# A graph-attention and mixture-of-experts layer: the last stage's three-way sum moved from ScalarE, GpSimd and VectorE to TensorE

## The reference

```
x = x + gnn(layernorm(x))                       # 4 heads of 64, 206,250 edges
x = x + ffn(layernorm(x))
# ffn: n = layernorm(x)
#   two experts of 16 per row, shares = softmax of the two gate values
#   moe = share0 * expert0(n) + share1 * expert1(n)
#   y   = n + moe
#   out = (y - mean(y)) / sqrt(var(y) + 1e-5) * gamma + beta
```

## Time and profile before

| | |
|---|---|
| runs | 2946.33, 2944.32, 2936.62 us; median 2944.32 us |
| profiled execution | 2945.44 us, its span 2943.7 us (first to last instruction) |
| mean granted TensorE clock | 0.796 of full speed |
| busy over the whole span | PE 76%, DVE 62%, POOL 64%, ACT 22% |
| expert stage ends (last matmul) | 2814.7 us from the span's start |
| last stage: first DMA issue to end of span | 2828.0 to 2943.7 us |

### The profile page before, as it was taken

How to read it: one execution, slowest core, us unless ns; L and a number is a source line. 1 busy time by engine, 2 the same in 40 slices (tenths; PEclk the granted TensorE clock), 3 DMA queues, 4 the chain that set the end, 5 groups by cost and what they waited for, 6 DMA issues and landing times. The chain is left out here.

```text
span 2943.7 us, 63652 instructions
## 1 busy us (share of the span) xinstructions
PE 2235.2 (76%) x10751; PEld 1884.9 (64%) x10752; DVE 1831.0 (62%) x4851; ACT 649.5 (22%) x2612; POOL 1887.7 (64%) x1912
## 2 busy tenths in 40 slices
PE   3588887888788888788787888887847368999920
PEld 2476776667666666666666766676637157999920
DVE  6666666666666666666666666666678851222258
ACT  1211111111111111111111111111112134555532
POOL 2277777777777777777777777777751344555533
PEclk9777778787778877887888788878875579999965
DMA  5355555555555555555555555555532056333356
GB/s 150 89 139 136 135 134 136 135 135 137 132 136 136 136 135 135 137 135 134 135 136 135 136 135 136 135 136 134 136 114 84 4 169 199 107 99 105 106 163 207
DMA packets 298512, 386.43 MB, mean 131 GB/s; under 512 B 104450, under 2 KB 235882, under 8 KB 298474
## 3 DMA queue, kind: packets, MB, share of 16 engines
q0 software_dynamic: 87744, 243.02, 31.9%
q10 hardware_dynamic: 84912, 75.49, 10.3%
q1 hardware_dynamic: 125818, 67.52, 8.3%
HBM read 351.08 MB, written 33.93 MB: 131 GB/s over the span
## 5 line engine op out<-in xcount | busy, mean ns | idle before, releaser
L552 POOL DMA_INDIRECT ring<-z_table,idx_ring x1612 | 1550.6, 962 | 495.6 <-issue 449.4
L738 PE MATMUL psMb<-msg,xs 128*128 128x260 f32 x3608 | 1208.2, 493 | 263.2 <-DVE msg L649 261.7
L738 PEld LDWEIGHTS psMb<-msg,xs 128*128 128x128 f32 x3608 | 829.1, 241 | 437.5 <-issue 271.3
L727 PEld LDWEIGHTS psEb<-nodes,xs 128*128 128x128 f32 x3608 | 566.4, 229 | 249.1 <-issue 214.8
L727 PE MATMUL psEb<-nodes,xs 128*128 x3608 | 532.8, 275 | 141.5 <-DVE xs L607 140.5
L649 DVE TENSOR_TENSOR msg<-ring,psPb 128x1024 f32<-128x1024 f32 x451 | 545.7, 1210 | 0.0
L621 DVE TENSOR_TENSOR earg<-es_edge,psEb 128x16 f32<-128x16 f32 x451 | 76.6, 170 | 604.2 <-ACT es_edge L699 599.2
L699 ACT COPY es_edge<-ring 128x16 f32 x451 | 91.9, 204 | 1493.4 <-SPq L523 1317.7
L613 DVE TENSOR_TENSOR xs<-iota_f,psPb 128x512 f32<-128x512 f32 x451 | 306.1, 679 | 1.4 <-ACT psPb L708 0.4
L607 DVE TENSOR_SCALAR xs<-dst_bc,iota_p 128x512 f32<-128x512 bf16 x451 | 231.7, 514 | 40.4 <-issue 20.4
L1224 DVE COPY xT<-psXd 128x256 f32<-128x256 f32 x108 | 45.8, 424 | 318.8 <-PE psXd L1158 318.8
(11 more groups left out here) (201 smaller groups left out, 1488.1 us busy)
## 6 DMA issues: line engine op xcount, KB each, us to landing
dst_bc<-dst_rows ACTq DMA_DIRECT2D x451, 128.0 KB
ring<-z_table,idx_ring POOLq DMA_INDIRECT x1612
w_all<-in_L_ffn_w_dram SPq DMA_DIRECT2D x32, 512.0 KB
b_sb<-in_L_ffn_b_dram ACTq DMA_DIRECT2D x108, 128.0 KB, 3.0
got<-pair_rows SPq DMA_DIRECT2D x48, 256.0 KB, 2.8
xs<-in_x_dram SPq DMA_DIRECT2D x6, 1536.0 KB, 13.8
idx_ring<-src_idx SPq DMA_DIRECT2D x403, 2.0 KB
z_table<-z_out SPq DMA_DIRECT2D x49, 130.0 KB, 1.9
```

The costliest lines, as they stand in the source:

```text
L552: nc.gpsimd.indirect_dma_start(ring[:, s, c, :], None, z_table, bass.IndirectOffsetOnAxis(ap=idx_ring[:, s, c:c + 1], axis=0)).then_inc(b_ ...
L727: last = nc.tensor.matmul(dest_of(s)[:, c * SH:(c + 1) * SH], ST[:, s, c * P:(c + 1) * P], nodes[:, bass.ds(tile, 1), :].rearrange("p o c ...
L738: last = nc.tensor.matmul(psM[s % 2][:, 0:ROW], S[:, s, c, :], msg[:, s, c, :], start=c == 0, stop=c == G - 1)
```

## The change

ACT no longer scales the rows. For each tile it makes two 128x128 matrices that hold the shares on their diagonals (`ident` times the share of each row, two activations at L1263 of the changed file). PE then makes the sum in PSUM with three float32 matmuls of 256 columns: diagonal 0 by the first expert's rows, diagonal 1 by the second's, and `ident` by the normed rows. There are two pairs of diagonals and four PSUM banks. DVE drops its addition and takes statistics and scale from PSUM; its statistics of tile t stand first in a turn, and `finish` follows `scale` directly. GpSimd has nothing left in the stage. SP's load waits for PE's sum in place of DVE's.

```
         with ExitStack() as ctx:
             got = sb(ctx, "got", [P, ER, TOP + 1, D])
             y = sb(ctx, "y", [P, ER, D])
+            diag = sb(ctx, "diag", [P, 2, TOP, P])
+            psS = [ps(ctx, f"psSe{i}") for i in range(4)]
...
-                def scale_first(t, s, r):
-
-                    act.wait_ge(e_got[s], 16 * 2 * (r + 1))
-                    nc.scalar.activation(got[:, s, 0, :], got[:, s, 0, :], ACT.Copy, scale=share[:, 0, bass.ds(t, 1)]).then_inc(e_first, 1)
-                pipeline(act, NT, ER, ER, [(scale_first, 0), (root, 3)])
-
-            @block.gpsimd
-            def _(pool):
-                def base(t, s, r):
-
-                    pool.wait_ge(e_first, t + 1)
-                    nc.gpsimd.tensor_tensor(got[:, s, 0, :], got[:, s, 0, :], got[:, s, TOP, :], ALU.add).then_inc(e_base, 1)
-                pipeline(pool, NT, ER, 0, [(base, 0)])
+                def spread_shares(t, s, r):
+
+                    if not early(t, 2):
+                        act.wait_ge(e_ps, t - 1)
+                    for k in range(TOP):
+                        last = nc.scalar.activation(diag[:, s % 2, k, :], ident[:, :], ACT.Copy, scale=share[:, k, bass.ds(t, 1)])
+                    last.then_inc(e_diag, 1)
+                pipeline(act, NT, ER, ER, [(spread_shares, 0), (root, 3)])
+
+            @block.tensor
+            def _(pe):
+                def combine(t, s, r):
+                    pe.wait_ge(e_diag, t + 1)
+                    pe.wait_ge(e_got[s], 16 * 2 * (r + 1))
+                    if not early(t, 4):
+                        pe.wait_ge(e_fin, 2 * (t - 4) + 2)
+                    for k in range(TOP):
+                        nc.tensor.matmul(psS[s % 4][:, 0:D], diag[:, s % 2, k, :], got[:, s, k, :], start=k == 0, stop=False)
+                    nc.tensor.matmul(psS[s % 4][:, 0:D], ident[:, :], got[:, s, TOP, :], start=False, stop=True).then_inc(e_ps, 1)
+                pipeline(pe, NT, ER, ER, [(combine, 0)])
...
-                def add_second(t, s, r):
-                    dve.wait_ge(e_base, t + 1)
-                    if not early(t, ER):
-                        dve.wait_ge(e_out[s], 16 * r)
-                    nc.vector.scalar_tensor_tensor(out=y[:, s, :], in0=got[:, s, 1, :], scalar=share[:, 1, bass.ds(t, 1)],
-                                                   in1=got[:, s, 0, :], op0=ALU.mult, op1=ALU.add).then_inc(e_sum, 1)
-
                 def tile_stats(t, s, r):
-                    dve.wait_ge(e_sum, 2 * t + 1)
-                    nc.vector.bn_stats(mv[:, s, 0:6], y[:, s, :]).then_inc(e_sum, 1)
+                    dve.wait_ge(e_ps, t + 1)
+                    nc.vector.bn_stats(mv[:, s, 0:6], psS[s % 4][:, 0:D]).then_inc(e_sum, 1)
...
-                pipeline(dve, NT, ER, ER, [(add_second, 0), (variance, 1), (invert, 2), (scale, 2), (tile_stats, 0), (finish, 2)])
+                pipeline(dve, NT, ER, ER, [(tile_stats, 0), (variance, 1), (invert, 2), (scale, 2), (finish, 2)])
...
                 def load(t, s, r):
                     if not early(t, ER):
-                        sp.wait_ge(e_sum, 2 * (t - ER) + 1)
+                        sp.wait_ge(e_ps, t - ER + 1)
```

More of the change, by code:

```diff
@@ L1241, in gnn_moe_kernel @@
         e_got = [sem(f"e_got{i}") for i in range(ER)]
-        e_sum = sem("e_sum"); e_fin = sem("e_fin"); e_var = sem("e_var"); e_root = sem("e_root")
-        e_first = sem("e_first"); e_base = sem("e_base"); e_y = sem("e_y"); e_out = [sem(f"e_out{i}") for i in range(ER)]
+        e_diag = sem("e_diag"); e_ps = sem("e_ps"); e_sum = sem("e_sum"); e_fin = sem("e_fin"); e_var = sem("e_var"); e_root = sem("e_root")
+        e_y = sem("e_y"); e_out = [sem(f"e_out{i}") for i in range(ER)]
         with ExitStack() as ctx:
@@ L1283, in variance @@
+                    nc.vector.bn_stats(mv[:, s, 0:6], psS[s % 4][:, 0:D]).then_inc(e_sum, 1)
                 def variance(t, s, r):
-                    dve.wait_ge(e_sum, 2 * t + 2)
+                    dve.wait_ge(e_sum, t + 1)
                     dve.sem_inc(apart, 1)
@@ L1292, in scale @@
                 def scale(t, s, r):
-                    nc.vector.scalar_tensor_tensor(out=y[:, s, :], in0=y[:, s, :], scalar=mv[:, s, 6:7], in1=affine[:, 0:D],
+                    if not early(t, ER):
+                        dve.wait_ge(e_out[s], 16 * r)
+                    nc.vector.scalar_tensor_tensor(out=y[:, s, :], in0=psS[s % 4][:, 0:D], scalar=mv[:, s, 6:7], in1=affine[:, 0:D],
                                                    op0=ALU.subtract, op1=ALU.mult).then_inc(e_fin, 1)
```

## The result

| | before | changed |
|---|---|---|
| median of 9 runs | 2944.32 us (2936.28 to 2949.18) | 2932.79 us (2927.24 to 2936.97) |
| ratio, 95% interval | | 0.9966 (0.9953 to 0.9979) |
| profiled execution, its span | 2945.44, 2943.7 us | 2927.24, 2925.5 us |

The change takes 11.5 us off the median. By the ratio it is 0.34%, 10.0 us, with an interval from 6 to 14 us. The forecast was 8.2 us, to 2937; that number starts from the profiled execution of 2945.44 us, and from the median the same 8.2 us give 2936.1. The same two kernels, compared once more (10 and 15 runs), gave 0.9960 (0.9948 to 0.9972).

The account below looks back on a forecast made before the run. VectorE was taken to bound the last stage at 2.084 us a tile, with SyncE's issues next. Start +0.5, steady part -9.0 and end +0.3 gave -8.2 us from 2945.44, so 2937 us, range 2929 to 2951.

Parts of the forecast that it names:

- forecast case: Last stage: turn of 1.80 to 1.92 us a tile, own range 2933 to 2941 us, chance 0.55.
- the rival in which DMA is the limit: Last stage: DMA engines, not SyncE's issues, set the pace at 1.72 us a tile, giving 2932 us; chance 0.15.
- the steady part: Last stage, 40 tiles going from 2.084 to 1.86 us each: 9.0 us less.
- VectorE bound, slowed by GpSimd: Last stage before: VectorE sets the pace, 1.64 us a turn with GpSimd idle, 0.44 more from overlap with GpSimd.
- SyncE is late next, at 1.84 us: Last stage after: SyncE's three DMA issues a tile set the turn, 1.84 us, bounds 1.75 to 1.95.
- DMA near its limit, so 0.02 more, 1.86: Last stage: DMA share would be 0.96 at 1.84 us, so 0.02 was added, making 1.86 us a tile.
- SyncE no limit: Last stage: SyncE's 0.71 us step contains a wait, DMA sets the pace at 1.72 us a tile, 2932 us; chance 0.15.
- VectorE's turn 1.34: Last stage: VectorE's turn without its addition, 1.24 us, plus 0.10 for finish waiting on scale; covered by SyncE.
- PSUM operands: VectorE's statistics and scale reading PSUM instead of SBUF: priced at 0, bounds -0.1 to +0.2 us a turn.
- TensorE's clock: Last stage: starts at 0.50, full some 5 us later and holds; at 0.50 again for the last tile.
- half-clock rival: Last stage: TensorE at half clock takes 2.67 us a tile, 2972 us; most or much of the stage, 2950 to 2972: 0.10.
- Start and end: Last stage: start priced +0.5 us (0 to +2), end +0.3 us (-1.1 if TensorE is at full clock).

Follow-up runs that it names:

- E3: Kernel before with GpSimd's addition of the normed rows left out, VectorE's addition kept, TensorE idle: 1.897 us a tile, stage 108.05 us.
- E5: Kernel before with GpSimd's addition of the normed rows done by VectorE, TensorE and GpSimd idle: 1.970 us a tile.
- E1: Changed kernel with the last stage's 49 stores issued by GpSimd instead of SyncE: 1.452 us a tile, stage 89.38 us, one run of 2920.96 us.
- E2: Changed kernel loading the normed rows of only 64 of 128 partitions, same count of DMA issues: 1.918 us a tile.
- E10: Changed kernel with GpSimd issuing stores, last tile split 96 and 10, VectorE's statistics between scale and finish: 1.360 us a tile, 0.9888 of the kernel before.
- E7: Changed kernel with only the first of TensorE's three matmuls a tile, all loads kept: 1.820 us a tile.
- E9: Changed kernel with only the first two of TensorE's three matmuls a tile, all loads kept: 1.835 us a tile.
- E4: Changed kernel with the last tile's loads and store split into 96 and 10 rows: load 48 to end 11.89 us against 20.91, 1.823 a tile.

## Why the prediction was right, and where its numbers were off

The median alone would not say so. At 2932.8 us it lies inside the whole range of 2929 to 2951, but just below the forecast case's own range of 2933 to 2941, and nearest to the 2932 of the rival in which DMA is the limit. The rows of the stage decide: SyncE's issues are the chain, and the stage is 9.3 us shorter where 8.2 were forecast. That 9.3 is so near to 8.2 is in part luck: the end, 0.6 us worse than forecast, hides part of the 1.6 us by which the steady part did better.

- **VectorE bound, slowed by GpSimd.** Right. E3 takes away only GpSimd's addition and gets 7.5 of 10.6 us; E5 shows the overlap as dearer than doing both additions in a row. Why the two engines slow each other, no run shows.
- **SyncE is late next, at 1.84 us.** Right in kind, shown by E1 (one issue less, pace 1.45) and supported by E2 (fewer bytes, no gain). The `ISA` row was priced at 0.06 us and was worth 0.10: 1.818 instead of 1.84. The turn without a jump, 1.76 us, is below the 1.80 to 1.90 that the prediction named as its sign and just above the 1.75 that it named as a sign of being wrong.
- **DMA near its limit, so 0.02 more, 1.86.** This step failed: no run shows the added term of 0.02 us a tile. The share of 0.85 at 2.084 us was scaled up as if 1.00 were a ceiling. E1 ran at share 1.06 and E10 at 1.08 and 373 GB/s, a pace of 1.36 us where the sum allowed 1.77, or 1.56 by the rate of loads alone. SyncE's turn, 0.02 us too long, and this 0.02 are the 0.04 us a tile by which 1.86 missed 1.818, and so the -9.0 that measured -10.6.
- **The rival "SyncE no limit".** Refuted in the direction of the forecast. The Trainium skill, "DMA: Bandwidth & Descriptors", section "Issuing engines are not separate DMA queues", has issue time as usually small beside the transfer. That did not hold in this stage: SyncE's turn of issues took 1.82 us, and the transfers of a tile can be done in 1.36 (E10).
- **VectorE's turn 1.34.** Too low. Finish right behind scale costs 0.61 us from start to start in the loop, not 0.50, and the turn is 1.48 (E1). It was covered by SyncE here; as soon as SyncE is relieved it is not, and the order of before gives 1.24 (E10). PSUM operands cost next to nothing: scale took 466 ns in the mean (494 before, some of them beside GpSimd) and the statistics 430 (414 before).
- **TensorE's clock.** As forecast: 0.50 at first, 1.00 four to five us later and through the steady part, 0.50 again for the last tile. The half-clock rival fell, and E7 says more: with SyncE at 1.82 us one matmul a tile at a level of 0.50 costs nothing, since it fits in. The Trainium skill, "TensorE: Matmul & The Clock Gate", section "A second HAM failure mode: psum-queue depth-cycling", has the clock swing in a kernel that goes round PSUM banks with short idle times. The changed kernel does that, four banks in turn with TensorE busy 81 to 87% of the time, and its clock did not swing; E9, with the same banks and less work, did. There the swing cost at most 0.015 us a tile; what it would cost with three matmuls, no run shows.
- **Start and end.** +0.40 against +0.5. The end +0.90 against +0.3: the last load took 10.1 us to TensorE's start instead of 9.6 to ScalarE's, and the rest of the work 6.4 us instead of 5.97, of which 6.1 to 6.3 were foreseen. E4 shows that both the late landing and the half clock could be avoided; the prediction took the landing as given.

## What to carry to other kernels

When the busiest engine of a stage is relieved, look at the turn of the queue that issues its DMAs before looking at bandwidth: find one turn in which it was behind and add up its steps; here that gave 1.85 us for a turn, and the floor after the change was 1.82. A DMA share near 1.00 in the profile is not a ceiling; only a run that issues faster shows the rate that is left. And moving an addition to an idle engine is not free: here doing both on one engine in a row (1.970 us a tile) was faster than one each at the same time (2.084).

## What the runs showed of the hardware

- VectorE's addition of 128x256 took 939 ns beside GpSimd's and 471 without; two additions alone, 1.970 us a tile, beat the split, 2.084.
- The share of the 16 DMA engines read up to 1.08, with 373 GB/s of mixed loads and stores in 1 KB rows; the same mix ran at 246 to 294 GB/s at shares of 0.82 to 0.96 in the kernels before and changed.
- A load of 106 partitions reached its user 10.1 us after issue, in pieces of 96 and 10 partitions 4.5 us after. A store of 106, alone under way, kept the 16 DMA engines 0.11 busy at 31 GB/s.
- Issuing a plain 128 KB store took GpSimd 0.54 us, SyncE 0.36.
- With one, two and three float32 matmuls of 256 columns in 1.82 us, TensorE's clock read 0.50, a swing with mean 0.92, and 1.00.
